# Decoder layer on one core: the values projected token by row, with x as the stationary operand

## What is computed

```python
q = (x @ Wq.T).reshape(b, s, 16, 128)
k = (x @ Wk.T).reshape(b, s, 4, 128)
v = (x @ Wv.T).reshape(b, s, 4, 128)       # 4 groups, 4 query heads for each
q, k = rope(q), rope(k)                     # v is not rotated
attn = softmax(q k^T / sqrt(128) + mask)
out  = (attn @ v) @ Wo.T
x    = layernorm(x + out)
```

## Time and profile before

| | |
|---|---|
| time, median of 3 runs | 355.08 us (354.58 to 357.39) |
| time of the profiled execution | 355.4 us |
| its span in the trace | 353.5 us |
| mean granted clock of PE | 0.983 |
| PE / DVE / ACT / POOL busy | 93% / 74% / 62% / 57% |
| attention part with its front | about 0 to 240 us |
| one unit of it | 27.6 us |

### The profile page before, as it was taken

One profiled execution on the slowest core, in us unless ns is written; L12 is line 12 of the kernel. 1 busy time (PEld: TensorE's weight loads), 2 busy tenths in 40 slices (PEclk: granted clock), 3 DMA queues, 4 the chain that ended last, 5 costly groups with the idle time before them and its releaser, 6 DMA issues.

```text
span 353.5 us, 6199 instructions
## 1 busy us (share of the span) xinstructions
PE 329.6 (93%) x2074; PEld 241.9 (68%) x2074; DVE 260.6 (74%) x500; ACT 217.5 (62%) x664; POOL 201.2 (57%) x284
## 2 busy tenths in 40 slices
PE   8978799999999999999999999999979999999982
PEld 3746688788778868868878877865556666566641
DVE  2774975874885884695794695799877889999545
ACT  3648457737756747656756656542336877777871
POOL 0487653765671783682685574299894468832012
PEclk9989999999999999999999999999969999999998
DMA  7911010023000004001004000000000000000000
GB/s 253 354 76 61 1 32 0 1 69 111 3 29 0 2 4 145 32 0 32 0 2 129 1 3 0 0 3 0 2 0 4 0 2 15 18 19 4 13 32 30
DMA packets 5615, 13.08 MB, mean 37 GB/s; under 512 B 848, under 2 KB 3024, under 8 KB 5328
## 3 DMA queue, kind: packets, MB, share of 16 engines
q1 hardware_dynamic: 5040, 11.90, 10.0%
q10 hardware_dynamic: 544, 0.79, 0.7%
HBM read 11.63 MB, written 1.05 MB: 36 GB/s over the span
## 4 chain that ended last, share of the span: by engine, by line
PE 71%; DVE 15%; POOL 5%; issue 4%; ACT 3%; DMA 1%; POOLq 0%; DVEq 0%
PE bank L365 12%; PE bank L495 12%; PE bank L396 8%; PE bank L382 7%; PE bank L484 5%; PE bank L659 4%; PE bank L648 4%; DVE toep L1092 4%; PE bank L614 3%; PE bank L473 3%; PE bank L669 2%; PE bank L643 2%; DVE t_cos L1056 2%; PE bank L623 1%; DMA x_raw<-in_xt 1%
## 5 line engine op out<-in xcount | busy, mean ns | idle before, releaser
L1498 POOL TENSOR_TENSOR prob<-prob,rden 128x512 f32<-128x512 f32 x32 | 33.6, 1051 | 68.7 <-DVE rden L1119 68.7
L1477 POOL TENSOR_TENSOR t_sin<-rot,sin 128x512 f32<-128x512 f32 x40 | 54.3, 1358 | 26.5 <-ACT rot L812 22.3
L842 ACT ACTIVATE prob<-bank,neg_max 128x128 f32<-128x128 f32 x128 | 45.2, 369 | 39.2 <-DVE neg_max L1112 39.2
L495 PE MATMUL bank<-wo_hi,head_hi 128*128 128x256 f32 x128 | 39.1, 305 | 1.8 <-DVE head_lo L1155 1.7
L396 PEld LDWEIGHTS bank<-k_rope,q_rope 128*128 128x128 f32 x256 | 34.2, 196 | 8.5 <-issue 3.3
L968 ACT ACTIVATE prob<-bank,fneg_max 128x128 f32<-128x128 f32 x128 | 36.7, 379 | 2.2 <-DVE fneg_max L1333 2.2
L396 PE MATMUL bank<-k_rope,q_rope 128*128 128x128 f32 x256 | 34.7, 280 | 2.6 <-DVE q_rope L1069 2.6
L365 PE MATMUL bank<-x_hi,w_hi 128*128 128x512 f32 x96 | 36.2, 458 | 0.9 <-ACT y L826 0.5
L495 PE MATMUL bank<-wo_lo,head_hi 128*128 128x256 f32 x128 | 36.0, 282 | 0.0
L495 PE MATMUL bank<-wo_hi,head_lo 128*128 128x256 f32 x128 | 36.0, 281 | 0.0
L1467 POOL TENSOR_TENSOR kv<-ctxT 128x256 f32<-128x256 f32 (+3 forms) x64 | 35.2, 585 | 0.0
(11 more groups left out here) (116 smaller groups left out, 759.9 us busy)
## 6 DMA issues: line engine op xcount, KB each, us to landing
w_raw<-in_wqkv SPq DMA_DIRECT2D x3, 768.0 KB, 5.1
toep<-in_toep SPq DMA_DIRECT2D x8, 256.0 KB, 3.4
wo_raw<-in_wo SPq DMA_DIRECT2D x4, 512.0 KB, 3.6
x_raw<-in_xt SPq DMA_DIRECT2D x2, 512.0 KB, 5.4
ctxT<-in_ctx SPq DMA_DIRECT2D x1, 1024.0 KB, 9.0
x<-in_x SPq DMA_DIRECT2D x1, 1024.0 KB, 9.2
out<-x SPq DMA_DIRECT2D x8, 128.0 KB, 1.7
wf<-in_wf SPq DMA_DIRECT2D x1, 784.0 KB, 4.6
```

Source lines behind the costliest of these rows:

```text
L495: last = pe.matmul(acc_bank[k // 2][:, (k % 2) * D:(k % 2 + 1) * D], hp[:, k % 2, h * P:(h + 1) * P], wp[:, 4 * v + h, :], start=(h + n == ...
L842: last = act.activation(prob[:, k % 2, h * P:(h + 1) * P], score_bank[k % 2][:, h * P:(h + 1) * P], ACT.Exp, bias=neg_max[:, k % 2, h:h + ...
L1477: pool.tensor_tensor(t_sin[:, par, :].rearrange("p (b t) -> p b t", b=BH), rot[:, par, :].rearrange("p (b t) -> p b t", b=BH), sin[:, :].u ...
L1498: pool.tensor_tensor(own, own, rden[:, k % 2, :].unsqueeze(2).to_broadcast([P, HG, P]), ALU.mult).then_inc(norm_done, 1)
```

## The change

V is projected directly with tokens on the partitions: for each of the four sequences, x (128 features by 128 tokens) is the stationary operand and the 128 weight columns of V are moving. That makes 4 sequences x 2 halves of the features x 3 products = 24 matmuls of 128 columns in place of six of 512. All 24 write the same PSUM bank that V had, 128 columns for each sequence. The transposes, the copy to `vT` and the two semaphores between them go; `copy_v` waits for the projection itself and stands where `copy_vT` stood, in the front and in the units. K and Q stay as they were.

```diff
-            def v_turn(u_next, out):
-
-                pe.wait_ge(vT_done, u_next + 1)
+            def project_values(j, out):
+
+                col = COLS.index("V") * P
                 for b in range(BH):
-                    last = pe.transpose(out[:, b * P:(b + 1) * P], vT[:, b * P:(b + 1) * P], ident[:, :])
-                last.then_inc(v_turned, 1)
+                    rows = slice(b * P, (b + 1) * P)
+                    for c in range(C):
+                        for n, (xp, wp) in enumerate(((x_hi, w_hi), (x_hi, w_lo), (x_lo, w_hi))):
+                            last = pe.matmul(out[:, rows], xp[:, j, c, rows], wp[:, c, col:col + P],
+                                             start=(c + n == 0), stop=(c == C - 1 and n == 2))
+                last.then_inc(proj_done, 1)
...
-                project(0, name, front_bank[name], first=(name == "K"))
+                if name == "V":
+                    project_values(0, front_bank[name])
+                else:
+                    project(0, name, front_bank[name], first=(name == "K"))
             keep_busy(16)
             scores(0, 0, 0)
             pe.wait_ge(in_ident, 16)
-            v_turn(0, front_bank["V"])
             scores(0, 0, 1)
...
-                        project(1 - j, name, item_bank(i))
+                        if name == "V":
+                            project_values(1 - j, item_bank(i))
+                        else:
+                            project(1 - j, name, item_bank(i))
...
                 item("V")
                 scores(u + 1, 1 - j, 1)
-                v_turn(u + 1, item_bank(BODY.index("V")))
                 output(3)
...
-            def copy_vT(bank_in, count):
-
+            def copy_v(u_next, j_next, bank_in, count):
                 act.wait_ge(proj_done, count)
-                act.copy(vT[:, :], bank_in[:, :]).then_inc(vT_done, 1)
-
-            def copy_v(u_next, j_next, bank_in):
-                act.wait_ge(v_turned, u_next + 1)
                 act.copy(v_tok[:, j_next, :], bank_in[:, :]).then_inc(v_done, 1)
...
                     if name == "V":
-                        copy_vT(item_bank(at), proj_count(u, at))
+                        copy_v(u + 1, 1 - j, item_bank(at), proj_count(u, at))
...
                 item("V")
                 if j == 0 and has_more:
                     split_w(v + 1, 1, proj_count(u, BODY.index("V")))
-                copy_v(u + 1, 1 - j, item_bank(BODY.index("V")))
                 exps(u + 1, 1)
```

## The result

The changed kernel is slower: 365.87 us median (365.61 to 369.25) against 355.29 us (354.58 to 357.39), ratio 1.031 with a 95% interval of 1.025 to 1.038. The forecast was 362.2 us. Its profiled execution has a span of 363.8 us, 10.3 us more than before.

What follows compares the result with a forecast made beforehand. PE was taken as the bound (93% busy, 71% of the chain). Terms: +6.2 us for PE in seven units, +1.2 for waits at Q1, -0.3 in the front: +7.1, so 362.2 us; range 357.5 to 383.

Steps and rivals of the forecast that it cites:

- rival A: V projection: short fp32r matmuls run at the fp32 pace, 0.222 us each; +25.9 us, so 381 us; chance 0.20.
- The case that came true: V projection: the load of 128 stationary columns sets the matmul pitch; +7.1 us, so 362.2 us; chance 0.60.
- The bound and the sign: Attention part: PE bounds, so its added time is very likely span; slower by over 1% was given 0.84.
- the detour: Each unit's chain leaves PE for VectorE (177.98 to 180.99), starting behind PE's `turn(1)`; claimed to hide nothing of longer V.
- The pitch: V projection: start-to-start distance of 128-column fp32r matmuls, set by their loads, taken as 0.113 us.
- B: V projection: load and stream run in series at 128 columns, 0.172 us each; +17.3 us, so 372 us; chance 0.04.
- C: V projection: cheaper loads, pitch below 0.093 us, so not slower; 353.3 us at 0.062; chance 0.13.
- the column theory: V projection: streamed columns alone would set the pitch, giving 0.062 us per matmul of 128 columns.
- PE in a unit: Each of seven units: 2.71 us of short matmuls added, 1.83 removed, +0.88 us; +6.2 us in all.
- The front: Before the units: longer projection fits PE's idle hole, clock may stay up; gain 0 to 0.6 us, 0.3 taken.
- ScalarE ... what follows V: Three weight-splitting units: PE reaches Q1 0.44 us sooner but waits for K's cosine product, 0.41 us each; +1.2 us.

Runs made afterwards that it cites:

- e5: The changed kernel with V projected in 48 matmuls of 64 columns instead of 24 of 128, twice the weight loads: 405.67 us (one run).
- e1: The changed kernel with one stricter GpSimd wait: Q0's sine product waits until VectorE has added K's rope; 362.25 us.
- e2: The changed kernel with the row maximum of step 1 ahead of the weights' low part on VectorE: 362.22 us.
- e8: The kernel before the change, with each sine product of the units waiting for the VectorE rope addition before it: 354.67 us, ratio 0.999.

## Why the prediction came out as it did

**The number.** 365.87 us lies in the stated range, 357.5 to 383, but that range was stretched to take in rival A, which is refuted. The case that came true had been given 360 to 364, and the measured time is 1.9 above it: 10.6 us were added, 7.1 were forecast. That the range held is luck; the terms below say which part of the reasoning held.

**The bound and the sign** held: PE carries the chain up to and through V, and the change is slower. But behind V, in a splitting unit, the chain now leaves PE for 8.65 us (181.07 to 189.72) where it had left it for 3 before; the prediction had taken the detour over as it was.

**The pitch** (0.113 us taken, 0.110 measured) held, and with it the choice between the far-apart bounds: the rows to go by were the loads with almost nothing streamed, not the fp32 products of 128 columns. Rivals A (0.222) and B (0.172) and C (under 0.093) are refuted by the records of the changed kernel, A and the column theory once more by e5.

The figure of 81 ns of the Trainium skill ("TensorE: Matmul & The Clock Gate", "Back-to-back issue gap") isn't what fp32r does here: 110 ns. The Trainium skill's section "LDWEIGHTS (loading the stationary operand)" on the same page gives a load as its columns divided by 1.2; for 128 columns that makes an estimate of 107 ns, and the trace agrees with 110 at the granted clock of 1.00. In e5 the same loads come 213 ns apart at 0.50, so there they don't follow it. The rule that the prediction took from that page's "The mechanism" in the Trainium skill, loads overlapping only with other row groups, doesn't hold for these 24 records: 0.110 us each, with load and stream over all rows. The same section of the Trainium skill also names a background weight buffer as a case in which a load is pulled ahead, which the prediction left out; no run tells whether these loads went there.

**PE in a unit** was +0.88 and is +0.85: the projection 0.80, and the scores behind it take 0.94 instead of 0.89.

**The front** was -0.3 and is -0.36. PE's idle hole before 22.8 us fell from 2.59 to 1.33 us, as forecast, and the clock stayed up behind it (1.00 instead of 0.59); that the one caused the other was not tested.

**The step that failed** is "ScalarE ... what follows V": the forecast saw that PE comes 0.44 us early to Q1 in the three splitting units, priced the wait at 0.41 (0.39 measured: 28.74 of e1 less 28.35 of e2), and stopped there. It asked who waits behind Q1 on PE, but not what happens on the engines that the earlier projections of K and Q0 feed. They fed ACT without a gap, ACT fed GpSimd without a gap, and the addition that had slipped into the gap lost its turn: 1.15 us more, three times, 3.4 us. With the measured terms the sum is 6 x 0.85 + 3 x 1.53 + 0.95 (from the last V on) - 0.36 (front) = 10.3 us, all of the difference of the spans. The warning stood in the trace of before, which the forecast hadn't read for this, as K's addition isn't in the chain of a unit. In the first unit, where ACT didn't idle either, GpSimd's two products stood as "x2" and the addition at 1.68 us already:

```profile
32.40 2.52 POOL L1477 TENSOR_TENSOR t_sin<-rot,sin 128x512 f32<-128x512 f32 x2
...
33.79 1.68 DVE L1069 TENSOR_TENSOR k_rope<-t_cos,t_sin 128x512 f32<-128x512 f32 x1 [1.49 <-POOL t_sin L1477]
```

Two durations of one instruction, 0.69 and 1.68 us, and a 0.22 us gap that decides between them.

## What to carry to other kernels

In these kernels an fp32r matmul at the full granted clock cost the longer of its stream and its load: 0.232 us with 512 columns and 0.119 with 256, but 0.110 with 128 and 0.111 with 64, each with a load of 128. So before projecting with the other operand stationary, count weight loads, not columns, and read their distance where hardly anything is streamed. When work goes from a bound engine, look at what its followers did in the gap that it left; an order between two engines that nothing enforces can flip and cost more than the work saved (1.15 us against 0.44 here), and one semaphore wait pinned it (e1). A longer duration of one and the same instruction beside another engine's is the place to look.

## What the runs showed of the hardware

**VectorE and GpSimd exclude each other when both work on SBUF tiles.** An addition of two SBUF tiles on VectorE took 0.69 us alone and 1.69 when GpSimd's product (1.28) began just ahead of it; the product took 1.72 when VectorE was first. VectorE's cosine product, which reads one operand from PSUM, kept its 0.69 us beside the same sine product (178.65, after). The Trainium skill says this of the port pair that they share ("SBUF — State Buffer", "SBUF: two separate sides"): whoever starts first holds it for the whole instruction. The trace agrees to about 0.15 us: the later of the two ended at 181.76 where the two one behind the other would end at 181.91 (after), and at 174.57 for 174.71 (before); and e1 turns the long addition into the short one by order alone.

**The clock can fall under a PE that never idles.** In e5 the granted clock went from 1.00 to 0.50 in the middle of back-to-back matmuls of 64 columns with a load each (PE busy 2.00 of 2.00 us), and the loads' distance from 0.111 to 0.213 us with it. The V projection of the changed kernel (24 matmuls, 2.63 us) keeps 1.00. What decides was not tested.

**The early third part is not steady.** Profiles of e1 and e2 differ there by 1.6 us, though no instruction of it differs; this can account for e2's missing 0.9 us (one profile of each was taken), and it is why the comparisons above go by units. Chain of e1, then of e2, from the score step (8 matmuls) to the next one:

```profile
259.65 1.11 PE bank L654 x8
...
277.03 0.86 PE bank L620 x2
...
279.23 1.06 PE bank L654 x8
```

```profile
258.81 1.11 PE bank L654 x8
...
276.44 1.71 PE bank L620 x2
...
280.01 1.06 PE bank L654 x7
```

PE idles ahead of it while the chain runs over GpSimd's products, and whether the value projection behind them (L620) meets the high or the low clock (0.86 or 1.71 us) changes from kernel to kernel; the granted clock of e2 from 272 to 280 us is 0.79. The single times of one kernel spread by about 1% (before, beside e8: 354.4 to 358.2); whether this is the reason was not tested.
